# Three parameter loads moved into the projection, and the last gather of the fourth block replaced by row fetches of SP, in a GRU over 200 steps

## What is computed

```python
x = emb[item_seq]; mask = item_seq != 0          # 512 x 200, D = 128, 12500 items
def step(h, inp):
    x_t, m_t = inp
    mx = x_t @ W + b_i                           # 128 -> 384
    mh = h @ U + b_r
    z = sigmoid(mx[:, :D] + mh[:, :D])
    r = sigmoid(mx[:, D:2*D] + mh[:, D:2*D])
    hh = tanh(mx[:, 2*D:] + r * mh[:, 2*D:])
    h_new = z * h + (1.0 - z) * hh
    return where(m_t[:, None], h_new, h), None
softmax(h_last @ Wout + bout)                    # 100 classes
```

## Time and profile before

| | us |
|---|---|
| median of 3 runs | 1031.94 (1031.76 to 1032.1) |
| profiled execution | 1033.86 |
| its span | 1032.0 |
| TensorE matmul busy | 979.4 (95%), 5218 instructions |
| VectorE busy | 789.6 (77%) |
| POOL busy | 764.2 (74%), 805 instructions |
| ScalarE busy | 588.3 (57%) |
| granted TensorE clock, mean | 0.989 of full |

### The profile page before, as it was taken

How to read it: one execution, slowest core, us unless ns; L and a number is a source line. 1 busy time by engine, 2 the same in 40 slices (tenths; PEclk the granted TensorE clock), 3 DMA queues, 4 the chain that set the end, 5 groups by cost and what they waited for, 6 DMA issues and landing times.

```text
span 1032.0 us, 20728 instructions
## 1 busy us (share of the span) xinstructions
PE 979.4 (95%) x5218; PEld 765.4 (74%) x5218; DVE 789.6 (77%) x2075; ACT 588.3 (57%) x1301; POOL 764.2 (74%) x805
## 2 busy tenths in 40 slices
PE   5999999999899989998999899999989999989887
PEld 4556888777677777776777777777768777766665
DVE  3444667888788878887888788788878888877777
ACT  2334555666566656665666566566656666655555
POOL 5677777777777777777777777777777777777774
PEclk9999999999999999999999999999999999999999
DMA  9997555555555555555555555555555555555553
GB/s 355 410 368 284 147 165 161 162 162 161 164 161 162 161 162 161 161 163 160 163 161 161 163 159 163 161 162 163 161 163 161 161 161 162 164 160 163 161 158 107
DMA packets 62715, 184.98 MB, mean 179 GB/s; under 512 B 16767, under 2 KB 20538, under 8 KB 62602
## 3 DMA queue, kind: packets, MB, share of 16 engines
q0 software_dynamic: 48448, 147.18, 49.3%
q1 hardware_dynamic: 12758, 35.83, 9.1%
q10 hardware_dynamic: 1396, 0.91, 0.3%
HBM read 157.78 MB, written 26.07 MB: 178 GB/s over the span
## 4 chain that ended last, share of the span: by engine, by line
PE 75%; POOL 11%; issue 6%; DMA 3%; DVE 2%; ACT 1%; SPq 0%; DVEq 0%; POOLq 0%; ACTq 0%
PE bank L470 20%; PE bank L476 13%; PE bank L472 13%; PE bank L458 12%; POOL arena L376 11%; PE bank L464 6%; PE bank L392 5%; DMA rows<-arena 2%; PE bank L439 1%; PE bank L444 1%; PE bank L440 1%; DVE h L647 1%; PE bank L397 1%; ACT cand L578 1%; DVE rh L642 1%
## 5 line engine op out<-in xcount | busy, mean ns | idle before, releaser
L376 POOL DMA_INDIRECT arena<-table,row_table x731 | 692.9, 948 | 223.1 <-issue 216.3
L576 ACT ACTIVATE bank<-bank,b_gates 128x256 f32<-128x256 f32 x400 | 179.5, 449 | 255.4 <-PE bank L476 255.4
L470 PE MATMUL bank<-h,U_sb 128*128 128x256 f32 x800 | 274.4, 425 | 18.6 <-DVE h L647 18.6
L657 DVE SCALAR_TENSOR_TENSOR bank<-bank,cand 128x256 f32<-128x256 f32 x400 | 172.8, 432 | 120.6 <-ACT cand L578 118.3
L578 ACT ACTIVATE cand<-pre,bi 128x256 f32<-128x256 f32 x400 | 202.9, 507 | 101.7 <-DVE pre L651 101.1
L458 PE MATMUL bank<-ident,arena 128*128 128x128 f32 x1496 | 228.2, 275 | 14.7 <-DMA arena<-table,row_table 14.4
L476 PE MATMUL bank<-h,U_sb 128*128 128x256 f32 x800 | 241.5, 384 | 0.0
L472 PE MATMUL bank<-h,U_sb 128*128 128x256 f32 x800 | 239.8, 381 | 0.0
L642 DVE SCALAR_TENSOR_TENSOR rh<-bank,br,r 128x256 f32<-128x256 f32 x400 | 193.6, 484 | 55.9 <-ACT r L574 33.4
L458 PEld LDWEIGHTS bank<-ident,arena 128*128 128x128 f32 x1496 | 184.9, 142 | 64.7 <-DMA arena<-table,row_table 31.4
L574 ACT ACTIVATE r<-bank,b_gates 128x256 f32<-128x256 f32 x400 | 189.9, 475 | 16.3 <-PE bank L470 14.4
(11 more groups left out here) (61 smaller groups left out, 248.4 us busy)
## 6 DMA issues: line engine op xcount, KB each, us to landing
arena<-table SPq DMA_DIRECT2D x2176, 1.5 KB
table<-arena SPq DMA_DIRECT2D x24, 768.0 KB, 4.9
arena<-table,row_table POOLq DMA_INDIRECT x731, 3.2
arena<-in_L_rec_emb SPq DMA_DIRECT2D x12, 512.0 KB, 10.3
rows<-arena SPq DMA_DIRECT2D x12, 512.0 KB, 10.7
raw<-rows,row_table POOLq DMA_INDIRECT x52, 4.7
seq<-in_r_item_seq ACTq DMA_DIRECT2D x1, 400.0 KB, 10.4
table<-arena SPq DMA_DIRECT2D x2, 192.0 KB
```

The lines of the kernel that those rows point to most:

```text
L376: pool.indirect_dma_start(ring_rows(s, k), None, table, bass.IndirectOffsetOnAxis(row_table[:, t, k:k + 1], 0)).then_inc(s_slot[s][c], 16)
L470: pe.matmul(reset_sum[c], U_sb[:, D:2 * D], h[c][:, :], start=False, stop=True, skip_group_check=True).then_inc(s_reset[c], 1)
L576: act.activation(update_sum[c], update_sum[c], ACT.Sigmoid, bias=b_gates[:, 0:1]).then_inc(s_z[c], 1)
L657: dve.scalar_tensor_tensor(out=update_sum[c], in0=update_sum[c], scalar=1.0, in1=cand[c][:, :], op0=ALU.subtract, op1=ALU.mult).then_inc(s ...
```

## The change

It has two parts.

First, ACT doesn't load U, Wout and bout at its start. It issues these three loads in the projection, ahead of its copy of piece 28. The loads of b_i and b_r stay.

Second, the rows of block 3 at step 199, the last one (slot 10, which is LEFT - 1), are no longer gathered by POOL. SP fetches them one at a time, behind its seventeenth block, with a semaphore of their own. POOL computes one more column of byte offsets, TensorE transposes 18 rows of offsets where it transposed 17, and the offsets of the second slow slot that SP brings onto one partition are 9 rows, the last of which is the new one. TensorE waits for all 128 row DMAs ahead of chain 1's transposes of the last step, and counts one gather fewer on the slot's semaphore.

```diff
+LAST_BLOCK = 3
-        slow_offsets = sb("slow_offsets", [P, 2 * TURNS + 1])
-        slow_turned = sb("slow_turned", [2 * TURNS + 1, P], I32)
+        slow_offsets = sb("slow_offsets", [P, 2 * TURNS + 2])
+        slow_turned = sb("slow_turned", [2 * TURNS + 2, P], I32)
+        s_last_block = sem("last_block_fetched")
@@ sync
-                sp.dma_start(slow_line[b:b + 1, 0:(TURNS + 1 - b) * P],
-                             slow_turned[b * (TURNS + 1):2 * TURNS + 1 if b else TURNS + 1, :]
+                sp.dma_start(slow_line[b:b + 1, :], slow_turned[b * (TURNS + 1):(b + 1) * (TURNS + 1), :]
                              ).then_inc(s_slow_line, 16)
@@ sync
             slow_block(0, TURNS)
+            for first in range(0, P, BATCH_ROWS):
+                offset = load_offsets(sp, 1, TURNS, first, BATCH_ROWS)
+                if first == 0:
+                    sp.wait_ge(s_free[1], (TURNS - 1) * RING + LEFT)
+                for i in range(BATCH_ROWS):
+                    sp.dma_start(ring_rows(LEFT - 1, LAST_BLOCK)[first + i:first + i + 1, :].bitcast(U8),
+                                 table_bytes[:, bass.ds(offset[i], ROW_BYTES)]).then_inc(s_last_block, 16)
@@ gpsimd
+            pool.tensor_scalar(slow_offsets[:, 2 * TURNS + 1:2 * TURNS + 2],
+                               row_f[:, LAST_BLOCK, STEPS - 1:STEPS], float(ROW_BYTES), None, ALU.mult
+                               ).then_inc(s_offsets, 1)
@@ gpsimd
-                        if (s, k) in SLOW:
+                        if (s, k) in SLOW or (t, k) == (STEPS - 1, LAST_BLOCK):
                             continue
@@ tensor
-                pe.wait_ge(s_slot[s][c], (turn + 1) * (16 * gathered) + (32 if s < RAW else 0))
+                last = isinstance(turn, int) and (turn, s) == (TURNS, LEFT - 1) and LAST_BLOCK in CHAINS[c]
+                pe.wait_ge(s_slot[s][c], (turn + 1) * (16 * gathered) + (32 if s < RAW else 0) - (16 if last else 0))
+                if last:
+                    pe.wait_ge(s_last_block, P * 16)
@@ scalar
-            for dst, src in ((U_sb, U), (bi, b_i), (br, b_r), (Wout_sb, Wout), (bout_sb, bout.partition_broadcast(P))):
+            for dst, src in ((bi, b_i), (br, b_r)):
                 act.dma_start(dst[:, :], src).then_inc(s_params, 16)
@@ scalar
             for i in range(CHUNKS, PIECES, 2):
+                if i == 2 * CHUNKS + AHEAD:
+
+                    for dst, src in ((U_sb, U), (Wout_sb, Wout), (bout_sb, bout.partition_broadcast(P))):
+                        act.dma_start(dst[:, :], src).then_inc(s_params, 16)
                 copy_proj(i)
```

More of the change, by code:

```diff
@@ L345, in _ @@
                                    ).then_inc(s_offsets, 1)
+            pool.tensor_scalar(slow_offsets[:, 2 * TURNS + 1:2 * TURNS + 2],
+                               row_f[:, LAST_BLOCK, STEPS - 1:STEPS], float(ROW_BYTES), None, ALU.mult
+                               ).then_inc(s_offsets, 1)
             pool.tensor_copy(row_table[:, :, :], row_f.rearrange("p k t -> p t k")).then_inc(s_idx, 1)
             pool.wait_ge(s_idx, 8)
-            pool.wait_ge(s_offsets, len(SLOW))
+            pool.wait_ge(s_offsets, len(SLOW) + 1)
             pool.wait_ge(s_pins, 2)
@@ L419, in _ @@
                 project(i)
-            slow_bank = bank[1][0:2 * TURNS + 1, 0:P]
-            pe.wait_ge(s_offsets, len(SLOW))
+            slow_bank = bank[1][0:2 * TURNS + 2, 0:P]
+            pe.wait_ge(s_offsets, len(SLOW) + 1)
             pe.wait_ge(s_tdve, CHUNKS + 1)
@@ L632, in _ @@
             dve.wait_ge(s_slow_turned, 1)
-            dve.tensor_copy(slow_turned[:, :], bank[1][0:2 * TURNS + 1, 0:P]).then_inc(s_slow_copied, 1)
+            dve.tensor_copy(slow_turned[:, :], bank[1][0:2 * TURNS + 2, 0:P]).then_inc(s_slow_copied, 1)
             dve.wait_ge(s_params, 16 * 5)
```

## The result

The changed kernel is slower: 1040.57 us (median of 6 runs, 1039.56 to 1042.75) against 1032.13 (6 runs, 1031.76 to 1032.72), a ratio of 1.0084 (95% interval 1.0073 to 1.0095), 8.4 us. The side was right and so was the mechanism, SP's late block. The size was not: 1037.1 was forecast, and the range ended at 1039.6.

What follows compares the result with a forecast made beforehand. POOL's gather stream was taken to bound the kernel before. SP's late added block would delay TensorE by 3.7 us and its fallen clock cost 1.5: 1031.94 + 3.7 + 1.5 = 1037.1 us, range 1034.9 to 1039.6.

Steps and rivals of the forecast that it cites:

- the saved gather: POOL's last gather, dropped at step 199: worth 0.37 us by itself, nothing under SP's late block.
- The rival taken from the Trainium skill's: SP's added block is in time and the kernel gains: 1030.7 us; chance 0.08.
- SP's first offset load: Start of SP's stream, to move ahead with the front by 0.9 us, ends 0.4 and 1.1.
- SP's seventeen blocks: SP's row fetches before the added block, taken from the earlier trace as 876.5 us, ending at 974.98 before the front's gain.
- the eighteenth block: SP's added 128 rows behind its seventeenth block, at the same pace: 50.55 us from block to block.
- landing of the last row: From the start of SP's last row issue to the row being there: 2.0 us, ends 1.5 and 3.1.
- the tail, slower clock: TensorE's clock falls after 4.95 us of idle before the last transposes: +1.5 us, ends 0 and 2.4.
- The rival of code fetched at run time: SP's added straight code is fetched while it runs, one stop of 3.0 us: 1040.1 us; chance 0.10.

Runs made afterwards that it cites:

- e1: The kernel before with only the three loads moved, the last block still POOL's gather; 1032.84 us, ratio 0.9984 to the kernel before.
- e3: The changed kernel, but SP fetches and TensorE awaits only 96 rows of the last block, the other 32 left out; 1033.03 us, ratio 0.9986.
- e2: The changed kernel with the three loads put back in the front, so only SP's added block remains; 1040.35 us, ratio 1.0055.
- e8: The changed kernel, but for block 3 of step 198 POOL gathers 32 rows and SP 96, step 199 all POOL's; 1031.89 us, ratio 0.9998.
- e7: The changed kernel with four matmuls of 128x384 in TensorE's idle ahead of piece 20 of the projection; 1039.12 us, ratio 1.0061.
- e9: The changed kernel with SP's loop written out as straight code; 1032.65 us, ratio 0.9985.
- e5: The changed kernel itself, run once more beside the kernel before; 1040.85 us, ratio 1.008.
- e11: The changed kernel with SP's loop written out, SP's block from step 198 in place of 199, and four matmuls in TensorE's front idle; 1031.11 us, ratio 0.9992.
- e6: The changed kernel with 16 useless matmuls on TensorE ahead of its wait for SP's last rows; 1039.36 us, ratio 1.0066.
- e4: The changed kernel with 20 useless matmuls on TensorE ahead of its wait for SP's last rows; 1040.94 us, ratio 1.0064.
- e10: The changed kernel with SP's loop written out and SP taking block 3 of step 198 in place of step 199; 1032.11 us, ratio 0.9977.

## Why the prediction failed in size

**Right.** POOL's stream set the end of the kernel before: e1, in which POOL starts 1.1 us earlier and SP does not, gains 1.5 us. The added block could not be hidden: from block to block it took 50.50 us (978.50 to 1029.00), where 50.55 was forecast. No gain from the saved gather shows (e3 against e1). POOL's stream began 1.07 us earlier, 0.9 was forecast. TensorE's clock fell, and the tail took 1.4 us longer than before the change, for 1.5 (10.8 us against 9.3; 1.0 to 1.7 over the profiles). That a long wait for a DMA drops the clock, and that the work after it starts slow, is what the Trainium skill's "TensorE: Matmul & The Clock Gate", section "HAM oscillation — how this bites in real kernels", says. This trace agrees: 0.50 in the window from 1026 us, 0.53 in the next. The rival taken from the Trainium skill's "DMA: Bandwidth & Descriptors", section "Issuing engine by pattern", that SP's DMAs are the faster way, fell: 50.50 us against a gather's 1.25.

**Wrong, by terms.** The transposes began at 1030.14 and not at 1026.35, 3.8 us later, in the profile of after:

| step of the sum | forecast | measured in after | difference |
|---|---|---|---|
| SP's first offset load | 98.5 - 0.9 = 97.6 | 98.6 | +1.0 |
| SP's seventeen blocks | 876.5 | 978.5 - 98.6 = 879.9 | +3.4 |
| the eighteenth block | 50.55 | 50.50 | 0 |
| landing of the last row | 2.0 | 1030.14 - 1028.8 = 1.4 | -0.6 |
| the tail, slower clock | 1.5 | 1.4 | -0.1 |

The first: "the projection and SP's stream" were to move ahead by 0.9 us. The first table store did land earlier, but TensorE had come to its wait earlier still; its idle grew from 2.2 us to 3.3, its clock fell to 0.57 from 40 us, and the projection gave back 1.7 us. Shown by e1 against e2, by e8, and by e7, where the filled idle brought SP's start to 97.5. The prediction weighed the clock in the tail, where it expected an idle, and never at the wait that it was itself making longer.

The second: the seventeen blocks had been read from one execution. They took 876.5 us there, 876.7 to 878.9 in e1 to e8, 879.9 in after. Of the 3.4 us more in after, 1.8 are in the stops at SP's six jumps back (19.5 us against 17.7 in all), which are gone in e9. The other 1.6 are in the blocks themselves, 1.0 of it in the first three, and why these took longer is open. The prediction's range had ends for the front, the landing and the clock, and none for this stream's length. The stream was followed by 54 us of waiting before, so its spread could not be seen in the time.

The third is arithmetic. The forecast put 5.2 us on the median of 1031.94, because the span was 1032.0. But a device time is 1.85 us more than its span in each run (1033.86 for 1032.0, 1042.75 for 1040.9), so that profile was of an execution 1.9 us slower than the median. Its POOL ran at the slower of two paces (below), which would make some 2 us; that this is the whole of it is likely, but not shown. SP's stream owes nothing to POOL's pace, and its end holds as it stands: 1026.35 + 9.3 + 1.5 + 1.85 = 1039.0 was the sum to make, 1.9 us above 1037.1 and inside the range. The other 1.6 us to 1040.57 are the rows of the table, with a stream of seventeen blocks as in e5 (976.9 - 98.9 = 878.0, +1.5) in place of after's: 1.0 + 1.5 - 0.6 - 0.1 = 1.8.

The rival of code fetched at run time named the right price, 1040.1, for a wrong place: the added straight code showed no stop (48.24 us for its 128 rows, 48.22 for the seventeenth block in the earlier trace rows). The stops of some 3 us were in the loop, six of them, and there already, so that the 876.5 us of the forecast held them.

## What to carry to other kernels

When work goes to a stream with slack, ask for its deadline and for its whole length: a block of 50.5 us did not fit into 54 us of wait, since that wait ran to the stores of the result at 1028.8, and the rows were needed, landed, 6 us earlier, at 1022.3 to 1022.7. Read such a stream's length from several executions, as its spread is hidden as long as it isn't the bound. And where a change makes an engine reach a wait sooner, look at the idle that it makes longer: TensorE can lose at its clock more than it gained.

## What the runs showed of the hardware

POOL's gathers run at one of two paces. The 731 of the earlier trace rows and those of e5 follow one another in 1.253 us, those of after and of e1 in 1.250:

```profile
L387 POOL DMA_INDIRECT arena<-table,row_table x730: 942/946/962, 103.6 to 1014.9; - x183
```

```profile
L387 POOL DMA_INDIRECT arena<-table,row_table x730: 945/949/960, 103.6 to 1017.3; - x183
```

The first is of after, the second of e5, the same program: 911.3 against 913.7 us over 729 steps. In the kernel before, that alone would move the time by 2.4 us. Of the thirteen profiles, after, e1, e2, e7, e8 and e11 have the faster pace. What sets the pace was not found.

Idles of TensorE of 1.83 (e2), 1.89 (e8) and 2.20 us (before) ahead of the projection left the clock full in the window from 40 us; those of 2.79 (e6) and 3.32 to 3.75 us (after, e1, e3, e4, e5, e9, e10) at the same place did not, and it was 0.50 to 0.67. The last row of 1.5 KB that SP fetched was there for TensorE 1.4 us after its issue began in after, e2, e5 and e7, where no other DMA of the kernel was under way, and 2.4 us in e10 and e11, beside POOL's gathers. A gather of 32 rows takes POOL 0.88 us and one of 128 rows 0.95. A load of 32 registers takes SP 2.04 us in the loop's program and 2.13 in the one written out.
